# Expert stage in 69 tiles of 256 rows instead of 37 of 512, second layer four steps behind the first, without a loop

## The reference

```
x = x + attention(layernorm_over_channels(x))      # 8 heads of 24, q and k normalised, softmax
t = tokens of x                                    # [16, 1024, 192]
n = layernorm(t)
p = softmax(n @ gate_w + gate_b)                   # 4 experts
mask = the two largest of p;  g = p*mask / (sum(p*mask) + 1e-9)
h_e = gelu(n @ w1[e] + b1[e])                      # 192 -> 768, exact gelu
y_e = h_e @ w2[e] + b2[e]                          # 768 -> 192
out = t + sum_e g_e * y_e
```

## Time and profile before

| what | us |
|---|---|
| median of three runs | 2649.07 |
| the profiled execution, its own time | 2650.99 |
| its span (first to last instruction) | 2649.3 |
| PE busy over the span | 2434.3 (92%) |
| ACT busy | 1772.7 (67%) |
| DVE busy | 1672.2 (63%) |
| POOL busy | 1426.0 (54%) |
| mean granted PE clock (1 is full) | 0.974 |

### The profile page before, as it was taken

The page is one execution under the profiler, slowest core; times in us unless marked ns, Lnnn a source line. Parts: engine busy times, 40 slices in busy tenths (PEclk is TensorE's granted clock), DMA queues, the critical chain, the costliest instruction groups (busy, mean ns, idle before and its releaser), DMA issues. The chain is left out here.

```text
span 2649.3 us, 53888 instructions
## 1 busy us (share of the span) xinstructions
PE 2434.3 (92%) x18693; PEld 1303.2 (49%) x18693; DVE 1672.2 (63%) x4869; ACT 1772.7 (67%) x2228; POOL 1426.0 (54%) x1137
## 2 busy tenths in 40 slices
PE   3799999999999999999999776999999999999975
PEld 2334334433433443343334224777777777777754
DVE  4657777876777787778678555555555555555522
ACT  2588788788778877887887653555565555656542
POOL 2434435543653564355445224777777777777750
PEclk9799999999999999999999987999999999999988
DMA  4221112112111221121121525444444444444429
GB/s 95 60 55 43 49 50 60 50 49 61 52 51 46 60 56 53 50 60 50 44 55 49 151 89 191 158 160 159 178 161 157 160 157 177 164 157 160 157 85 336
DMA packets 160323, 275.25 MB, mean 104 GB/s; under 512 B 21812, under 2 KB 129828, under 8 KB 150676
## 3 DMA queue, kind: packets, MB, share of 16 engines
q1 hardware_dynamic: 141700, 244.65, 28.7%
q0 software_dynamic: 13392, 27.97, 2.9%
q10 hardware_dynamic: 5056, 0.42, 0.2%
HBM read 173.29 MB, written 49.69 MB: 84 GB/s over the span
## 5 line engine op out<-in xcount | busy, mean ns | idle before, releaser
L818 ACT ACTIVATE probs<-ps_s 128x1024 f32<-128x1024 f32 x1024 | 1008.5, 1023 | 213.3 <-PE ps_s L717 210.0
L1371 POOL TENSOR_TENSOR h_split<-h_f,h_split 128x512 f16<-128x512 f32 x444 | 552.4, 1244 | 236.7 <-ACT h_f L1348 229.6
L1344 ACT ACTIVATE h_split<-ps_h,packs 128x512 f16<-128x512 f32 x444 | 305.2, 687 | 391.0 <-PE ps_h L1298 391.0
L1298 PE MATMUL ps_h<-m_xn_t,packs 128*128 128x512 f16 x2220 | 553.5, 380 | 0.5 <-DVE m_xn_t L1433 0.5
L730 PE MATMUL ps_o<-probs,v_aug 128*32 128x512 f32 x4096 | 547.0, 606 | 1.2 <-DVE o_sb L844 0.9
L1084 POOL TENSOR_TENSOR inv_norm<-sumsq,minus_half 128x16 f32<-128x16 f32 x128 | 380.6, 2973 | 273.7 <-DVE sumsq L1027 273.4
L1312 PE MATMUL ps_y<-packs,h_split 128*128 128x192 f16 x5328 | 511.9, 245 | 0.6 <-POOL h_split L1371 0.6
L1312 PEld LDWEIGHTS ps_y<-packs,h_split 128*128 128x128 f16 x5328 | 453.1, 97 | 105.1 <-POOL h_split L1371 1.0
L717 PE MATMUL ps_s<-even 98*128 98x512 f16 x1024 | 300.6, 383 | 12.7 <-ACT probs L818 10.9
L717 PE MATMUL ps_s<-stacks_odd 98*128 98x512 f16 x1024 | 298.4, 382 | 13.3 <-ACT probs L818 11.1
L1348 ACT ACTIVATE h_f<-ps_h,packs 128x512 f32<-128x512 f32 x444 | 302.0, 680 | 0.0
(11 more groups left out here) (213 smaller groups left out, 2806.4 us busy)
## 6 DMA issues: line engine op xcount, KB each, us to landing
packs<-expert_pack SPq DMA_DIRECT2D x74, 1635.0 KB, 6.9
even<-heads SPq DMA_DIRECT2D x192, 96.0 KB, 2.4
stacks_odd<-heads SPq DMA_DIRECT2D x192, 96.0 KB, 2.4
tile_rows<-sorted_rows SPq DMA_DIRECT2D x37, 400.0 KB, 6.6
tokens<-in_x_dram SPq DMA_DIRECT2D x16, 768.0 KB, 5.5
y_in<-y_tokens SPq DMA_DIRECT2D x16, 768.0 KB, 8.7
out_dram<-y_out SPq DMA_DIRECT2D x16, 768.0 KB, 6.7
even<-heads SPq DMA_DIRECT2D x128, 48.0 KB
```

Source lines behind the costliest of these rows:

```text
L818: act.activation(probs[:, u % PRING, :], ps_s[:, u % 2, :, :].rearrange("p f n -> p (f n)"), ACT.Exp).then_inc(s_probs, 1)
L1298: mm = pe.matmul(ps_h[:, n % HBUF, :], w1(par, slot, w, k), xn_t[0:rows_k, par, c, :], start=(i == 0), stop=(i == 4))
L1344: act.activation(h_split[:, n % HSPLIT, 0, :], ps_h[:, n % HBUF, :], ACT.Gelu, bias=bias1(par, slot, k), scale=1.0 / WSCALE)
L1371: pool.tensor_tensor(h_split[:, n % HSPLIT, 1, :], h_f32[:, n % HBUF, :], h_split[:, n % HSPLIT, 0, :], ALU.subtract).then_inc(s_h, 1)
```

## The change

`SLOT` becomes 2, so a tile has 256 rows, and `NTILE` becomes (16384 + 6 * 255) // 256 = 69. Each step has five first-layer matmuls of 256 columns and six second-layer matmuls of 192. The second product runs four steps behind the first. `ps_h` has five banks in place of three, `ps_y` two in place of four, `h_split` eight buffers, `h_f` five. The numbers of the steps in which the jobs stand move. `token` has three buffers, and the wait ahead of the token copy is for writes of an earlier tile. The row loads and the padding fill halve in size; the packs do not change in size and are still two per tile. All programs are written out for all tiles, without a loop. Buffer numbers go by the running step number, since 12 is no multiple of 5 or 8.

```diff
-SLOT = 4
+SLOT = 2
...
-LAG = 2
-HBUF, HSPLIT = 3, 4
-XN_AT, CAST_AT, SUB_AT, N_AT = 3, 4, 5, 6
-ACC_AT, ADD_AT, SCATTER_ROWS_AT = 9, (8, 2), 4
+LAG = 4
+HBUF, HSPLIT, TBUF = 5, 8, 3
+XN_AT, CAST_AT, SUB_AT, N_AT = 2, 3, 5, 7
+ACC_AT, ADD_AT, SCATTER_ROWS_AT = 9, (10, 4), 6
...
-    token = sb("token", [P, 2, SLOT], I32)
+    token = sb("token", [P, TBUF, SLOT], I32)
...
-    ps_h = ctx.enter_context(nc.psum_tensor("ps_h", [P, HBUF, TROWS], F32))
-    ps_y = ctx.enter_context(nc.psum_tensor("ps_y", [P, 2, 2, 512], F32))
+    ps_h = ctx.enter_context(nc.psum_tensor("ps_h", [P, HBUF, 512], F32))
+    ps_y = ctx.enter_context(nc.psum_tensor("ps_y", [P, 2, SLOT // 2, 512], F32))
...
-            mm = pe.matmul(ps_h[:, n % HBUF, :], w1(par, slot, w, k), xn_t[0:rows_k, par, c, :],
+            mm = pe.matmul(ps_h[:, (STEPS * tile + n) % HBUF, 0:TROWS], w1(par, slot, w, k), xn_t[0:rows_k, par, c, :],
...
-                if not (isinstance(tile, int) and tile < 1):
-                    dve.wait_ge(s_put, 16 * SLOT * (tile + 1))
-                dve.tensor_copy(token[:, nxt, :], rows[:, nxt, :, ID]).then_inc(s_token, 1)
+                if tile + 1 >= TBUF:
+                    dve.wait_ge(s_put, 16 * SLOT * (tile + 3 - TBUF))
+                dve.tensor_copy(token[:, (tile + 1) % TBUF, :], rows[:, nxt, :, ID]).then_inc(s_token, 1)
...
-            pe_tile(pe, 0, 0)
-            with pe.Fori(0, NTILE // 2 - 1) as i:
-                for k in range(2):
-                    pe_tile(pe, i * 2 + 1 + k, 1 - k)
-            pe_tile(pe, NTILE - 2, 1)
-            pe_tile(pe, NTILE - 1, 0)
+            for tile in range(NTILE):
+                pe_tile(pe, tile, tile % 2)
...
```

More of the change, by code:

```diff
@@ L1311, in second_product @@
             for i, (hp, wp) in enumerate(((0, 0), (0, 1), (1, 0))):
-                mm = pe.matmul(y, h_split[:, n % HSPLIT, hp, tok], w2(par, slot, wp, k),
+                mm = pe.matmul(y, h_split[:, (STEPS * tile + n) % HSPLIT, hp, tok], w2(par, slot, wp, k),
                                start=(k == 0 and i == 0 and t % 2 == 0), stop=(k == NK - 1 and i == 2),
@@ L1343, in act_tile @@
                 act.wait_ge(s_w2, STEPS * tile + n - HSPLIT + 1)
-            act.activation(h_split[:, n % HSPLIT, 0, :], ps_h[:, n % HBUF, :], ACT.Gelu, bias=bias1(par, slot, k),
+            act.activation(h_split[:, (STEPS * tile + n) % HSPLIT, 0, :], ps_h[:, (STEPS * tile + n) % HBUF, 0:TROWS], ACT.Gelu, bias=bias1(par, slot, k),
                            scale=1.0 / WSCALE)
@@ L1347, in act_tile @@
                 act.wait_ge(s_h, STEPS * tile + n - HBUF + 1)
-            act.activation(h_f32[:, n % HBUF, :], ps_h[:, n % HBUF, :], ACT.Gelu, bias=bias1(par, slot, k),
+            act.activation(h_f32[:, (STEPS * tile + n) % HBUF, :], ps_h[:, (STEPS * tile + n) % HBUF, 0:TROWS], ACT.Gelu, bias=bias1(par, slot, k),
                            scale=1.0 / WSCALE).then_inc(s_gelu, 1)
@@ L1357, in put_rows @@
     def put_rows(pool, tile, par, t):
-        pool.indirect_dma_start(mlp.y_tokens[:, :], bass.IndirectOffsetOnAxis(ap=token[:, par, t:t + 1], axis=0),
+        pool.indirect_dma_start(mlp.y_tokens[:, :], bass.IndirectOffsetOnAxis(ap=token[:, tile % TBUF, t:t + 1], axis=0),
                                 y_sb[:, par, t, :], None).then_inc(s_put, 16)
@@ L1370, in pool_tile @@
                     pool.wait_ge(s_w2, STEPS * tile + n - HSPLIT + 1)
-                pool.tensor_tensor(h_split[:, n % HSPLIT, 1, :], h_f32[:, n % HBUF, :], h_split[:, n % HSPLIT, 0, :],
+                pool.tensor_tensor(h_split[:, (STEPS * tile + n) % HSPLIT, 1, :], h_f32[:, (STEPS * tile + n) % HBUF, :], h_split[:, (STEPS * tile + n) % HSPLIT, 0, :],
                                    ALU.subtract).then_inc(s_h, 1)
@@ L1472, in _ @@
         def _(act):
[L1473 to L1478, removed]
+            for tile in range(NTILE):
+                act_tile(act, tile, tile % 2)
         @block.gpsimd
@@ L1485, in _ @@
             pool.dma_start(mlp.y_tokens[B * NTOK:B * NTOK + P, :], y_sb[:, 1, 0, :]).then_inc(s_put, 16 * SLOT)
[L1486 to L1491, removed]
+            for tile in range(NTILE):
+                pool_tile(pool, tile, tile % 2)
             pool_tile(pool, NTILE, 1, main=False)
@@ L1497, in _ @@
             dve_tile(dve, -1, 1, main=False)
[L1498 to L1503, removed]
+            for tile in range(NTILE):
+                dve_tile(dve, tile, tile % 2)
             dve_tile(dve, NTILE, 1, main=False)
```

## The result

The changed kernel takes **2583.73 us** (median of 4 runs, 2582.28 to 2585.79). The kernel before takes 2648.05 us beside it (4 runs, 2644.75 to 2651.59). The ratio is 0.9757, 95% interval 0.9745 to 0.9770: 64 us or 2.4% faster. The profiled execution took 2584.04 us with a span of 2582.3; the span before was 2649.3, so the traces differ by 67.0 us.

The account below looks back on a forecast made before the run. PE was taken to bound the expert stage. Savings of 59 + 1.5 + 3.2 + 2 = 65.7 us off 2650.99 give 2585.3; with the median 1.9 lower, the forecast is 2584 us (range 2574 to 2597).

Parts of the forecast that it names:

- the main term: PE in the expert stage: 69 tiles of 12.8 us, 884 us against 943, remove 59 us (54 to 67).
- Rival 4: PE's weight loads are not hidden: 1530 more at 85 ns add 130 us, giving 2714 us; chance 0.01.
- The room argument: Between first and second product, four steps leave about 2.0 us; POOL is up to 1.64 us late, so no stall.
- rival 1: POOL late for the second product: 0.2 to 0.6 us per tile, 14 to 41 us, 2598 to 2625 us; chance 0.24.
- The pack chain: Pack issue, landing, `start_acc` and `add_expert` before PE reuses slot 0's bank: 10.9 of 13.35 us, 2.5 left.
- two groups of 1.1, half of 2.27 each: DVE's `start_acc` after a pack lands: each of its two groups was put at half the earlier 2.27 us.
- rival 2: Expert packs come too late and bound the tile: costs from a 9.4 us landing; 2700 us at 11; chance 0.08.
- its sign of being wrong: Pack landing times over 9 us would make the prediction wrong.
- rival 3: Expert stage code must be fetched: 81 pieces, a stall of one piece each is 89 us, 2673 us; chance 0.03.
- The edges: Outside the steady expert tiles: savings of 1.5 us at its start, 3.2 at its end and 2 in setup.
- The longer tile table: Tile table of 414 elements, not 222: at most 4 us, beside POOL's last indirect writes, so nothing.
- The setup block: POOL's 20.3 us wait for padding writes, which halve: saves 0 to 6 us, taken as 2.

Follow-up runs that it names:

- tiles_74: The changed kernel with 74 tiles of 256 rows, as many rows (18,944) as the kernel before computed: 2651.36 us, ratio 1.0005.
- after_again: The changed kernel, unchanged, timed on another occasion as a comparison on the same chip: 2586.61 us, ratio 0.9759.
- loop_kept: The changed kernel with the loop kept, four first-layer banks and buffers in place of five, and two token buffers: 2587.22 us, ratio 0.9763.
- pack_late1: The changed kernel with the load of each tile's second pack issued one step (1.04 us) later: 2586.53 us, ratio 0.9762.
- tiles_alone: The kernel before with only SLOT = 2 (69 tiles), keeping its loop, two steps between products, three banks and step numbers: 2661.27 us, ratio 1.0049.
- pack_late3: The changed kernel with the load of each tile's second pack issued three steps (3.1 us) later: 2683.56 us, ratio 1.0123.
- before_unrolled: The kernel before with its four loops written out, tiles and lag unchanged: 2650.65 us, ratio 1.0005.

## Why the prediction was right

The time came out at 2583.7 against 2584, and by the mechanism forecast. (The sum gives 2583.4: 2585.3 less 1.9. The forecast rounded it up.) Point by point:

**PE's work, the main term.** 56.4 us against 59. The matmul of 256 columns takes 108 to 109 ns, the tile 12.82 us; 69 tiles are 884.6 and 37 of before were 943.1, a difference of 58.5. The rest of the stretch took 5.2 us in after and 3.1 in before, which the sum did not have. 1.9 of the 5.2 are the one tile of 14.7 us; filling and tail are 3.3 and 3.1. tiles_74 shows where the term comes from: five tiles more bring 64.0 us back. The rows alone would give more than 58.5, and the small tiles take some of it, as the prediction had said.

**Weight loads.** 7512 loads, 660 us of PEld, run under 698.5 us of PE. If 1530 more had been paid, tiles_74, which has 28% more pairs than before (74 x 138 = 10,212 against 7992), would have shown it first; it takes the same time. Rival 4 is out.

**ACT and POOL.** The groups by shape, 1700 to 2400 us of after, with busy us and mean ns:

```profile
L1371 POOL TENSOR_TENSOR h_split<-h_f,h_split 128x256 f16<-128x256 f32 x655 | 451.3, 702 | 123.0 <-ACT h_f L1348 120.0
L1344 ACT ACTIVATE h_split<-ps_h,packs 128x256 f16<-128x256 f32 x654 | 310.4, 475 | 151.5 <-PE ps_h L1298 146.5 <-issue 5.0
...
L1396 DVE SCALAR_TENSOR_TENSOR acc<-packs,tile_rows,acc 128x192 f32<-128x192 f32 x110 | 95.7, 909 | 1.9
L1396 DVE SCALAR_TENSOR_TENSOR acc<-packs,tile_rows 128x192 f32<-128x192 f32 x110 | 89.8, 855 | 109.8 <-DMA packs<-expert_pack 109.8
```

ACT takes 475 ns (taken: 450, bounds 344 to 487). POOL's subtraction takes 702 on average, of which the clean ones 0.67 (taken: 0.66). POOL is busy 557 of 700 us, 80% and not 89%: the 0.9 us per tile that I had added for DVE are mostly in the 702 ns already, and 12 x 0.70 + 2 x 0.98 is 10.4 us. The room argument held where it was put: four steps suffice and three don't. The waits of after in the same 700 us, where rival 1 would show:

```profile
PE ps_y L1312 <- POOL h_split L1371: 1.5, 2, 0.8
```

Both are in one tile, and there rival 1 did happen:

```profile
2354.41 0.97 POOL L1359 DMA_INDIRECT y_tokens<-y_sb,token  x1 [2.73 <-PE ps_y L1312]
...
2356.22 0.67 PE L1312 MATMUL ps_y<-packs,h_split 128*128 128x192 f16 x6 [0.81 <-POOL h_split L1371]
...
2358.15 0.67 PE L1312 MATMUL ps_y<-packs,h_split 128*128 128x192 f16 x6 [0.72 <-POOL h_split L1371]
```

POOL stood 2.73 us ahead of a write of rows, more than the room of 2.0, and PE lost 1.9 us once (14.71 between two row loads instead of 12.83). after_again, tiles_74, loop_kept and pack_late1 have such a tile at the same place. What held POOL is open.

**The pack chain: right in its verdict, wrong in its size.** I had left it 2.5 us of room; it has 1.2. The timelines of SP, DVE, POOL and PE over the half tile that matters, in after:

```profile
1706.74 0.34 SPq L1285 DMA_DIRECT2D packs<-expert_pack  x1
...
1713.34 1.75 DVE L1396 SCALAR_TENSOR_TENSOR acc<-packs,tile_rows 128x192 f32<-128x192 f32 x2 [1.41 <-DMA packs<-expert_pack]
1715.12 2.08 DVE L1396 SCALAR_TENSOR_TENSOR acc<-packs,tile_rows,acc 128x192 f32<-128x192 f32 x2
1717.24 0.74 DVE L1382 SCALAR_TENSOR_TENSOR acc<-ps_y,gate_w,acc 128x192 f32<-128x192 f32 x2
...
1713.43 3.56 POOL L1371 TENSOR_TENSOR h_split<-h_f,h_split 128x256 f16<-128x256 f32 x5
...
1719.20 0.66 PE L1312 MATMUL ps_y<-packs,h_split 128*128 128x192 f16 x6
```

The pack is issued at 1706.74 and is there 6.6 us later, at 1713.34 (taken: 6.9). `start_acc` lasts until 1717.2, 3.9 us where the sum had 2.2. `add_expert` ends at 1717.98, and PE needs the bank at 1719.20. The step of the prediction that is mis-sized is "two groups of 1.1, half of 2.27 each". The 2.27 were not four equal pieces of work. What a group of two costs by itself is seen in tiles_alone, on DVE and POOL:

```profile
1709.06 1.48 DVE L1396 SCALAR_TENSOR_TENSOR acc<-packs,tile_rows 128x192 f32<-128x192 f32 x2
1710.57 0.75 DVE L1396 SCALAR_TENSOR_TENSOR acc<-packs,tile_rows,acc 128x192 f32<-128x192 f32 x2
...
1708.25 2.07 POOL L1371 TENSOR_TENSOR h_split<-h_f,h_split 128x256 f16<-128x256 f32 x3
1711.17 0.68 POOL L1371 TENSOR_TENSOR h_split<-h_f,h_split 128x256 f16<-128x256 f32 x1 [0.85 <-ACT h_f L1348]
```

Beside POOL's three subtractions two instructions take 1.48 us; in POOL's pause, from 1710.32 to 1711.17, two take 0.75, so 0.41 each with their overlap. Now POOL in the kernel before, at the time of the group of the earlier trace rows:

```profile
1868.71 1.16 POOL L1371 TENSOR_TENSOR h_split<-h_f,h_split 128x512 f16<-128x512 f32 x1 [0.33 <-ACT h_f L1348]
1870.94 1.16 POOL L1371 TENSOR_TENSOR h_split<-h_f,h_split 128x512 f16<-128x512 f32 x1 [1.08 <-ACT h_f L1348]
```

DVE's four instructions began at 1868.80 beside one subtraction, which ended at 1869.87. The first of them ended at 1870.08 and took 1.28 us; the other three took 0.41 each in POOL's pause. So the 2.27 us were one meeting with POOL and three pieces of work, and a meeting lasts until POOL's instruction ends, however few instructions the group has. In after the pack lands just behind the second write of rows, when POOL makes good its lateness with five subtractions back to back and leaves no pause. There all four instructions meet one: they take 1.00, 0.82, 1.33 and 0.82 us (the timeline read instruction by instruction), and each ends 0.21 or 0.22 us after the end of a subtraction. In pack_late3, where the pack lands after the catching up, every second one is free: 0.42 and 0.83, twice.

The four terms 0.9 + 6.6 + 3.9 + 0.7 are 12.1 of the 13.35 us. With 3.9 in place of 2.2 rival 2 has a price once the pack of slot 1 lands in more than about 7.8 us (an estimate from these terms), where the prediction said 9.4, and its sign of being wrong, landings over 9 us, was set too high as well. pack_late1 (fits) and pack_late3 (doesn't) bracket this.

**DMA.** Queue 1 in 1700 to 2400 us, and the pack issues, which answer to the earlier trace rows:

```profile
q1 hardware_dynamic: 23525, 193.38, 77.6%
...
packs<-expert_pack SPq DMA_DIRECT2D x109, 1635.0 KB, 6.6
```

77.6% where 77 was forecast, and 294 GB/s where 293 was. Twice the traffic didn't lengthen the median landing (6.9 before), so rival 2 did not set in. DVE waits for packs 109.8 us in 700, but PE does not wait for DVE.

**Fetching code.** before_unrolled rules out rival 3 as a price on every piece (1.1 us each): its whole loss is the one stall of 0.8 us. The changed kernel's own waits name no stall for code.

**The edges.** The start of the stage gave 1.0 and not 1.5: DVE's half is shorter as forecast (0.67 for two normalisations at 1605.47, 1.25 for four in the earlier trace rows), but PE then waits 2.49 us for the first pack, where it had waited for DVE. The longer tile table costs nothing, as forecast: from the start of the last image's routing to the first normalisation 28.6 us pass in both kernels. The end gave 3.8 against 3.2. The setup block gave 3.9 against 2: the padding writes halve and the wait for them shrinks from 20.3 to 16.1 us. Over all traces it is 2.2, so the term was right and this pair of executions an extreme one. Forecast less measured, the errors are +0.5 for the start, -0.6 for the end, -1.9 for the setup block, +2.6 for the main term, and -2.0 for the stretches that I had put at nothing (attention and output). They nearly cancel, so that the total is nearer to the truth than its terms is luck.

## What to carry to other kernels

Where one engine is full, count its work first: here 6.8% fewer rows, all of them padding, gave the whole gain of the stage, and the same tiles with the old number of rows gave none. Smaller tiles shorten every deadline while fixed costs (a write of rows, a pack's landing, a meeting of DVE with POOL) stay, so work out the room of each chain in steps, and put the products as many steps apart as the slowest helper can be late: two steps lose 74 us (with three banks and the old step numbers), three lose 23, four nothing but the 1.9 us of one tile. When a step is moved to free a path, charge it to the queue that it enters: the earlier start with the bias writes ahead of the weight loads cost 13 us (2599.36 against 2586.61), and with them behind the stores it gained about 6.

## What the runs showed of the hardware

- The DVE instructions of this stage that read only SBUF wait for a busy POOL. The two-input instructions of L1396 take 0.41 us where POOL pauses and 855 and 909 ns on average in after. One that meets a subtraction ends 0.21 to 0.23 us after that subtraction's end, in before, in after and in pack_late3. Beside POOL's five subtractions in a row they take up to 1.33 us (the longest of the stage 1.96), while POOL's own take 0.66 to 0.81. It is not only instructions with two inputs: the cast of L1425 takes 0.36 us at 1606.17, with POOL idle, and 0.82 on average in mid-stage. DVE's `add_expert`, which has an input from PSUM, keeps its 0.74 for two (1.38 for four in the earlier trace rows). The Trainium skill, page SBUF — State Buffer, section SBUF: two separate sides, says that a DVE instruction with two SBUF inputs and a GpSimd instruction that reads SBUF share one pair of ports, which the first holds for the whole instruction while the other blocks. The trace agrees for DVE: four instructions take 3.9 us beside five subtractions, and each ends just behind one. POOL lost little in turn, since five subtractions in 3.56 us are 0.71 each where a clean one takes 0.67; why it is spared, no run here tells.
- Weight loads of 128 x 128 are hidden under matmuls of 192 and 256 columns at 7512 loads in 698.5 us. PE's time is the columns: 83, 108 and 214 ns for 192, 256 and 512.
- A pack's landing did not grow with the traffic: 1635 KB took 6.9 us at a DMA share of 0.45 and 6.6 at 0.83. It depends more on when the issue comes: 6.5 to 8.2 us over the variants. The 8.2 are those of pack_late3, at a share of 0.70, where the two packs of a tile are issued 3.5 us apart (1706.16 and 1709.62), so that their loads overlap.
- Code without a loop cost PE at most 0.8 us in 700, at 47 pieces, and nothing that its waits name at 60.
